# Fourteen row buffers in place of eight for the gathers of an edge loop, in a graph network kernel on one core

## The reference, cut to what matters

```
xs0, xs1 = h0[edge_src], h1[edge_src]          # gather: one row of h (256 floats) for each edge
hid = silu(edge_length_embedded @ fc_w0 / sqrt(8))
w = hid @ fc_w1 / sqrt(64)                     # weights of each edge
midA = wA * xs0 * sh0 ; midB, midC, midD ...   # products of weights, rows and edge attributes
y = segment_sum(mid, edge_dst)                 # sum over the edges of each destination
```

## Time and profile before

| | |
|---|---|
| time, median of 3 runs | 3951.65 us (3951.26 to 3953.61) |
| span of the profiled execution, first to last instruction | 3966.1 us |
| own time of the profiled execution | not measured apart from its span |
| the edge loop: first gather to last product | 2648.0 to 3349.9 us of the span |
| busy in the whole span | PE 3642.8 us (92%), DVE 2451.9, ACT 1491.9, POOL 665.9 |
| gathers | 392, 375.4 us of POOL |

### The profile page before, as it was taken

The page is one execution under the profiler, slowest core; times in us unless marked ns, Lnnn a source line. Parts: engine busy times, 40 slices in busy tenths (PEclk is TensorE's granted clock), DMA queues, the critical chain, the costliest instruction groups (busy, mean ns, idle before and its releaser), DMA issues. The chain is left out here.

```text
span 3966.1 us, 60201 instructions
## 1 busy us (share of the span) xinstructions
PE 3642.8 (92%) x18935; PEld 3087.8 (78%) x18935; DVE 2451.9 (62%) x4843; ACT 1491.9 (38%) x3475; POOL 665.9 (17%) x658
## 2 busy tenths in 40 slices
PE   5999899999999999999996999988888888869996
PEld 2555699999999998999994888657777777848885
DVE  7886655555555555556554666556666665677775
ACT  0363311211211111112114544457777775136663
POOL 0002000000000000000002200025555553012221
PEclk9999999999999999999997999989999999879998
DMA  1353022222222222222222210112222222431113
GB/s 53 65 105 65 26 87 89 65 89 84 70 84 74 80 88 71 83 83 71 83 69 98 72 31 30 42 47 83 81 84 79 84 80 59 150 71 38 38 38 119
DMA packets 265216, 288.48 MB, mean 73 GB/s; under 512 B 70331, under 2 KB 237327, under 8 KB 264283
## 3 DMA queue, kind: packets, MB, share of 16 engines
q1 hardware_dynamic: 233701, 208.44, 18.1%
q0 software_dynamic: 24192, 66.15, 5.8%
q10 hardware_dynamic: 7030, 10.16, 0.7%
HBM read 242.21 MB, written 42.48 MB: 72 GB/s over the span
## 5 line engine op out<-in xcount | busy, mean ns | idle before, releaser
L1043 PE MATMUL bank<-a_wide,parts 125*128 125x448 f32 x4200 | 872.9, 367 | 0.0
L1043 PEld LDWEIGHTS bank<-a_wide,parts 125*128 125x128 f32 x4200 | 785.6, 188 | 78.4 <-issue 9.9
L2288 POOL DMA_INDIRECT rows<-h_dram,src_t x392 | 375.4, 958 | 331.9 <-DVE prod L2483 218.7
L2421 ACT ACTIVATE hot<-eq,ea 128x80 f32<-128x80 f32 x1568 | 405.3, 352 | 1.0 <-DVE eq L2463 0.5
L1093 DVE CAST a_wide<-a_cols 125x2240 fp32r<-125x2240 bf16 x210 | 275.5, 1328 | 138.7 <-PE bank L1043 138.7
L1017 POOL TENSOR_TENSOR nf_g<-nf,nf_g 128x896 fp32r<-128x896 f32 x42 | 95.4, 2271 | 1575.0 <-ACT nf_g L1187 1575.0
L2328 PEld LDWEIGHTS bank<-prod,hot 128*80 128x80 f32 x2352 | 295.9, 153 | 70.9 <-issue 21.6
L2328 PE MATMUL bank<-prod,hot 128*80 128x128 f32 x2352 | 331.8, 277 | 10.6 <-issue 10.4
L1052 PE MATMUL bank<-nf_g,whh 128*128 128x448 f32 x1512 | 339.7, 369 | 0.0
L1052 PE MATMUL bank<-msg,wc 128*128 128x448 f32 x1512 | 339.1, 369 | 0.0
L1052 PEld LDWEIGHTS bank<-msg,wc 128*128 128x128 f32 x1512 | 284.2, 188 | 27.5
(11 more groups left out here) (438 smaller groups left out, 5787.7 us busy)
## 6 DMA issues: line engine op xcount, KB each, us to landing
a_cols<-a_dram SPq DMA_DIRECT2D x210, 546.9 KB
a_dram<-a_cols SPq DMA_DIRECT2D x15, 1250.0 KB, 9.9
w<-in_w SPq DMA_DIRECT2D x4, 2728.0 KB
deg_bc<-deg_dram SPq DMA_DIRECT2D x42, 224.0 KB, 6.0
gate_bc<-gate_dram SPq DMA_DIRECT2D x42, 224.0 KB, 3.2
rows<-h_dram,src_t POOLq DMA_INDIRECT x392
w<-y_rows SPq DMA_DIRECT2D x12, 512.0 KB, 15.1
w<-in_w SPq DMA_DIRECT2D x6, 896.0 KB
```

The lines of the kernel that those rows point to most:

```text
L1043: ins = nc.tensor.matmul(p_msg[f][:, 0:GW], parts[0:SPB, m, c * HB + k, f * 128:(f + 1) * 128], a_wide[u % 2][0:SPB, k, :], start=(c == 0 ...
L2288: nc.gpsimd.indirect_dma_start(out=rows[n % ITC][:, :], out_offset=None, in_=h_dram, in_offset=bass.IndirectOffsetOnAxis(ap=src_t[:, n:n + ...
L2421: ins = nc.scalar.activation(hot[:, q % 2, j, m, :], eq[:, q % 2, j, :], ACT.Copy, scale=ea4[:, q * UC + j, m:m + 1])
```

## The change

The edge loop of `edge_convolution` gets ROWS_AHEAD = 14 buffers and 14 gather semaphores in place of ITC = 8, and POOL waits for the products of chunk n - 14. The six buffers take 6 KB more in each partition. DMAS becomes 28 * 16 (392 chunks over 14). In `adjacency` ACT clamps the number of rounds at zero with one more register instruction for each tile.

```diff
+ROWS_AHEAD = 14
@@ adjacency, ACT
                 ranges_at, turns, _, rounds = begin(act, "act")
+                more = act.alloc_register("a_more_act")
...
-                        act.reg_add(turns, turns, rounds)
+                        act.reg_alu(more, rounds, 0, ALU.max)
+                        act.reg_add(turns, turns, more)
@@ edge_convolution
-                                  *(f"c_gathered{j}" for j in range(ITC)))
+                                  *(f"c_gathered{j}" for j in range(ROWS_AHEAD)))
-        rows = [sb(ctx, f"rows{j}", [EC, D]) for j in range(ITC)]
+        rows = [sb(ctx, f"rows{j}", [EC, D]) for j in range(ROWS_AHEAD)]
-        DMAS = NIT * 16
+        DMAS = NCH // ROWS_AHEAD * 16
@@ POOL
-                        pool.wait_ge(p_done, chunks + n + 1 - ITC)
+                        pool.wait_ge(p_done, chunks + n + 1 - ROWS_AHEAD)
                         pool.sem_inc(passed, 1)
                         nc.gpsimd.indirect_dma_start(
-                            out=rows[n % ITC][:, :], out_offset=None, in_=h_dram,
+                            out=rows[n % ROWS_AHEAD][:, :], out_offset=None, in_=h_dram,
...
-                        ).then_inc(gathered[n % ITC], 16)
+                        ).then_inc(gathered[n % ROWS_AHEAD], 16)
@@ DVE
-                        dve.wait_ge(gathered[n % ITC], dmas + n // ITC * 16 + 16 - START)
+                        dve.wait_ge(gathered[n % ROWS_AHEAD], dmas + n // ROWS_AHEAD * 16 + 16 - START)
                         dve.wait_ge(w_mm, chunks + n + 1)
-                        x, w = rows[n % ITC], p_w[j][0:EC, :]
+                        x, w = rows[n % ROWS_AHEAD], p_w[j][0:EC, :]
```

## The result

The changed kernel takes 3960.04 us (median of 12 runs, 3956.16 to 3964.01) against 3951.74 us for the kernel before on the same chip (12 runs, 3949.82 to 3956.67). The ratio is 1.0021, 95% interval 1.0012 to 1.0029: 8.3 us slower, with 4.7 to 11.5 us as the interval. The mark of 0.2%, which the prediction set between no change and slower, lies inside that interval. The forecast of 3955.3 lies 4.7 us under the median, and its ratio of 1.0009 just under the interval. Rival B's 3960.8 is within 1 us of what was measured.

A forecast was written before the change was run, and what follows sets the result against it. The prediction took the loop to be near PE's pace, with PE's signals late while gathers stream. Start +5, end -1.4, middle and rest 0 gave +3.6 us on 3951.65, so 3955.3 us, range 3925 to 3965.

The forecast's parts named there:

- Rival B: Loop start: all 7.5 us of the longer first stream on the path, 3 us more for PE's clock; 3960.8 us, chance 0.22.
- That the rows are not what DVE waits for: Edge loop: gathered rows lie ready about 2 us after issue; DVE's 198.4 us of waits are for PE's late signal.
- Rival A: Edge loop: DVE waits for the rows, so fourteen buffers save up to PE's 90.1 us idle; 3861.6 us, chance 0.12.
- the three views: Evidence against late rows: DMA engines already silent, ACT and SP let go with DVE, waits ending 1.40 us after POOL's last gather.
- That PE is late while gathers stream, and comes through when the stream pauses: Edge loop: PE's completions reach other engines late during streaming gathers, over 4 us in one wait, until POOL hits its limit.
- Middle of the loop, 0: POOL reaches its limit at either lead, then each product frees one gather as now; 0 us change.
- The upper bound of 90.1 us: Edge loop: PE's total idle time ahead of its four matmul groups, taken as the most any change to gathers could save.
- Start of the loop, +5: First stream six gathers longer, 7.5 us, with DVE let go behind it; 5 us slower, bounds 0 and 7.5.
- End of the loop, -1.4: Last gather is freed six products earlier, so six more chunks pass without a stream; 1.4 us faster.
- The rest, 0: DVE's waits, DMAS, ACT's added instruction in adjacency, six more semaphores to clear and buffer addresses; 0 us.
- Its bound of 24 us: Most that ACT's added register instruction in adjacency, executed 79 times and bounded by 0.30 us each, could cost if uncovered.
- rival D: Start and end of the loop cost 0, no change at all; 3951.7 us, chance 0.58 together with the forecast.

The follow-up runs named there:

- the seven stretches: Kernel with fourteen buffers, lead eight, the loop cut into 56-chunk stretches that differ in how rows are fetched; 3939.92 us on chip D against 3955.11 before.
- limit8_all: Changed kernel with its fourteen buffers, but POOL held to eight chunks ahead as before; 3949.54 us, ratio 0.9996 to the kernel before.

## Why the forecast came out as it did

**That the rows are not what DVE waits for: right.** The wait moved from gather n + 7 to n + 13 with the lead, leads from five to fourteen give middles (product 20 to 360) between 590 and 606 us, with no gain from a longer lead (five: 595.9; eight: 589.9 and 605.8; fourteen: 591.6), and the same bytes brought by SP make no wait of over 0.6 us. Rival A is out. One of the three views was misread, though. The strip of the earlier trace rows does not fall silent at 2762.4: its slices are 0.24 us long and the last busy ones of that burst, 8, 6 and 2, run from 2762.1 to 2762.8. So a gather is through some 2.4 us after its start and not 2, and the data of the last gather arrive in the moment in which DVE is let go, not before it (in the profile after they arrive 1.5 us before). The silent engines, on which the prediction also rested its 0 for the middle, were no argument for it. What carries the reading is that this last gather is that of chunk n + 7, and that ACT and SP are let go too.

**That PE is late while gathers stream, and comes through when the stream pauses: right in the main, on this chip, and its first half is shown by the seven stretches.** The mechanism was read too narrowly in one respect. I took PE to have done its work and only its signal to be late. The timeline after shows PE itself starting single instructions 2.1 us apart beside the stream, with nothing named that it waits for. How much is late signals and how much late starts stays open. About a fifth of the waits end within the issue of a gather, so a pause is the rule and no condition. And the prediction took it for a trait of the kernel; on chips B, C and E it is not there at all, and the change is worth 0 (0.9999 on C). Nothing in the one profile of before tells that another chip would differ.

**Middle of the loop, 0: right, as far as can be told.** From product 20 to 360 the changed kernel takes 591.6 us and limit8_all 589.9; the profile of before took 605.8 at the same lead as limit8_all, so one execution tells this to some 15 us, and it is the medians of the whole kernel that leave no room for a gain. DVE's waits of over 1 us come to 202.9 us in 83, where I had said near 220, and POOL's to 192.3 us, where I had said some 200. The upper bound of 90.1 us, PE's idle time, was too small. On chip D the stretch without gathers is 0.20 to 0.30 us a chunk shorter than those with a wait for each gather, 77 to 116 us for 392 chunks, and PE gets less done even while it is busy: 455 matmuls in 61.52 us against 544 in 70.00 (a matmul's end is modelled). Rival A's time hung on that bound.

**Start of the loop, +5: the term that was mis-sized.** It measured 40.11 - 32.91 = 7.2 us against limit8_all by product 20, and 6.1 against the profile of before. The step that failed is "I take 5, nearer the upper end, because all the waits shown ended behind the stream": the reason given was one for the upper end itself. A signal that passes during the stream, on which the lower bound rested, did not pass this time: DVE made four products before the stop, not five. The forecast's signs came in: 18 gathers where I said about 19, the stream's end at 2671.81 (near 2672), DVE let go at 2674.72 (near 2674). Rival B had said 7.5 us and 3 us more for the clock. The clock was indeed at 0.50 for over 4 us beyond 2674, so its second part is in the trace. Its size was not measured by itself, and by the 7.2 us at product 20, clock included, the two parts together are smaller than B's 10.5.

**End of the loop, -1.4: right in sign.** From product 360 to 391 it is 48.3 us against 50.2, -1.9 us in one execution each.

**The rest, 0: right.** limit8_all carries all of it, at a ratio of 0.9996. Its bound of 24 us had no good ground: it took the 0.30 us between gathers for a wait and a semaphore instruction, and the stretch with one wait for four shows 0.30 us without either.

**The sum.** 7.2 - 1.9 = +5.3 us by the traces, with +7.0 from first to last product. The runs say +8.3 (4.7 to 11.5) against before. The 1 to 3 us between are within that interval, and a loop in a single execution is no steadier: it took 683.5 and 701.9 us in two kernels whose medians differ by 2.4 us. This also explains the one sign of mine that failed, 702 to 709 us for the loop: it took 690.5. I had scaled it to the loop of a profile that was itself 14.45 us over its median.

So the forecast holds by its range and by every sign but that one, and its point value is 4.7 us short. The start accounts for 2.2 of these, less 0.5 for the end; the rest is not resolved. B, at 0.22, came nearer in its total than the forecast, though its two parts for the start are together larger than what was measured. And the terms of the sum belong to the slower kind of chip: on C the same change is worth 0, as rival D had it.

## What to carry to other kernels

A deeper prefetch is not free where issuing the prefetch disturbs the engine that bounds the loop: the gathers moved ahead cost about their full issue time, 7.5 us for six, whether all at the start or spread, and are paid back only in part at the end. Before giving a wait more buffers, see who else is let go in the same moment; two engines that need no rows and wake together with the one that does tell more than the name in the bracket. And compare a loop's time with that of a second execution before building on it, on a second chip if there is one.

## What the runs showed of the hardware

- Two levels of time for one program, by chip or by the chip's state at the time: 3952 to 3955 us (the first, A and D) and 3841 to 3844 us (B, C and E). The difference lies in the loop with gathers; it runs at 1.65 to 1.77 us a chunk on the one and 1.45 on the other, while with no gathers issued chip D does 1.453 too.
- On D, of the first kind, PE loses 6.6 to 8.5 us of 70 while GpSimd issues indirect DMAs with a wait for each, whether these move 18 or 85 GB/s, and 11.5 with one wait for four, and loses none beside SP's plain copies at 96 GB/s.
- A gather of 128 rows occupies GpSimd 1.25 us from start to start, with one wait and one increment, with three increments, and with neither, and for 128 bytes a row as for 1 KB.
- What in the chip holds PE up was not found. In the 16 us around the longest stall no code was being loaded, and the data of the last gather were through 1.5 us before it ended.
